# Attention in two passes, routing inside the second, and a recurrence whose input is added on VectorE

## The chip, the cores and the metric

The kernel runs on one core of one Trainium2 chip. The core has five engines with a queue each, which work side by side and wait for each other by semaphores: TensorE (PE in the profile; PEld is its loading of weights), VectorE (DVE), ScalarE (ACT), GpSimd (POOL) and SyncE (SP), which here only issues transfers. SBUF is the on-chip memory of 128 partitions, PSUM the memory that TensorE writes its sums to. The metric is device time in microseconds of one execution. Lower is better.

## The reference

Two layers over `x` of 4 x 2048 x 256 float32. What matters, cut:

```python
# layer 0
xn = layernorm(x); u = layernorm_w(xn) @ (Ws + Wi).T + bs + bi
h[t] = tanh(h[t-1] @ A.T + u[t])                 # 16 states, 2048 steps, per batch row
s = (h @ Wo.T + bo) * sigmoid(layernorm_w(xn) @ Wg.T + bg) + xn
g = silu(small per-feature MLP of xn)
x = x + s * g
# layer 1
xn = layernorm(x); q, k, v = xn @ Wq.T + bq, xn @ Wk.T + bk, xn @ Wv.T + bv
s = softmax_one(causal(q k^T / 4)) @ v           # 16 heads; it attends over the FIRST axis, the batch of 4
g = silu(MoE(xn))                                # 8 experts, top 2, capacity 2048, hidden 1024
x = x + s * g
```

The attention's sequence axis is the first one, so each of the 2048 positions attends among its 4 batch rows, and scores are ten products per position (4 + 3 + 2 + 1). The mixture gives each token's two experts a slot; the slot is the token's rank among the tokens that chose the expert, so a slot can be known only when all 8192 tokens have logits.

## The kernel before

All data of a stage is cut along the positions into NT = 16 tiles of 128 positions by 4 batch rows (1024 columns per partition). The stages are blocks with a barrier between them, each with an instruction list per engine written out by hand:

- `prepare`: loads and folds weights.
- `mix`, first loop: normalise, transpose, the recurrence's input `u_st`. Second loop (16 tiles): gate product `a_pG` (line 718), small MLP (lines 726, 728), output gates. Into its gaps the recurrence is woven: the 2048 steps are cut into 128 chains of 16, swept three times, which makes SWEEPS * L = 48 steps; slots 0 to 3 of the first twelve tiles take one each. A step is an identity product that copies `u_st` into PSUM (line 700), a product with the block-diagonal A added to it (703 or 706), and ScalarE's tanh into `h_st` (633). VectorE has no part in a step. Its list per tile: four instructions on the gate product (569), `finish` of the tile before (555, 557, 560), `normalise` (540), `units` (548).
- `recur`: more sweeps, only if the third one changed the last state.
- `attend`, one loop over 16 tiles, software-pipelined. `layer0(t)` on VectorE (956 to 972): layer 0's output times the gate, added to `x_st`, and its statistics. GpSimd's `scale` (909 to 917) makes the factors, ScalarE normalises (1046), SyncE stores the rows to HBM, TensorE turns them (1124), and from the turned tile makes Q (into `pY`), K (`pX`), the router's logits (1147) and V (`pY`). VectorE, for tile t: `layer0(t + 2)`, four products q * k (1003), four reductions to scores (1009), maximum (1014), subtraction (1017); then it waits for ScalarE's exponential (1096); sum, plus one, reciprocal, and `c_att` (1021 to 1029). GpSimd multiplies `c_att` by the values and adds, seven instructions per tile (936, 942) with a `scale` between them.
- `route`: a stage of its own, nearly all of it one list on VectorE: constants; `best`, `first`, one-hot of each token's two experts (1273 to 1282, the second choice without the lines for k == 0); a scan along the positions (1284); two TensorE products that count over partitions; places and slots (1291 to 1309); then 16 groups of three instructions over 128 x 1024 bfloat16 elements which write a slot's high part, low part and code as one-hots (1316 to 1319), each group followed by eight TensorE matmuls that add it into the table `d_ptab` (1351); last the table's decoding (1323 to 1333). SyncE meanwhile loads the first expert's weights.
- `experts`: 8 experts by 4 groups of 512 slots, gathered and scattered by GpSimd's indirect transfers.
- `combine`: the last gate and the store.

The order of each list is fixed, so an instruction waits for all ahead of it on its engine.

## Time and profile before

| | us |
|---|---|
| median of 3 runs | 1430.29 (1430.05 to 1431.13) |
| the profiled execution | 1429.75 |
| its span, first to last instruction | 1427.9 |
| mean granted TensorE clock | 0.935 of full |

| engine | busy us | share of the span |
|---|---|---|
| TensorE | 1175.3 | 82% |
| VectorE | 1016.6 | 71% |
| ScalarE | 628.1 | 44% |
| GpSimd | 625.2 | 44% |

The page shows these as rows, and the span in forty slices of 35.7 us, a digit for the busy tenths of each:

```profile
PE   4899999588888884146999989999899998999910
DVE  7757667759888887885767667676576765776638
POOL 5500000028777777013454544645546455464430
PEclk9999999799999997557999999999999999999965
```

Mix ends in the eighth slice, attention fills the next eight and a half, routing follows at half clock (5), and the experts begin at the end of the eighteenth. A view by windows gives the busy time of each engine in a stretch; a timeline gives the instructions in order of time, merged where neighbours are alike: start, duration from the first one's start to the last one's end, engine, line, what is written from what, the count, and in brackets the idle time before it with what ended it. A duration includes the time an instruction is held back once its engine has started it.

### The profile page before, as it was taken

To read this page: it belongs to the slowest core of one execution; us is meant where nothing else is said; L and a number is where in the kernel's file an instruction comes from. 1 tells how busy PE (TensorE), PEld (TensorE's weight loads), DVE (VectorE), ACT (ScalarE), POOL (GpSimd) and SP (SyncE) were. 2 spreads that over 40 slices of the span, in tenths; PEclk is the share of its full clock that TensorE was granted. 3 is DMA by queue.
4 is the path that set the end of the run, shared out by engine and by line. 5 is a ranking of instruction groups with operands and counts; after the bars stand their busy time and mean duration, and the time that the engine had idled before them with its cause. 6 is when DMAs were issued, how large, how long until landed. Compare 5 with 4: busy or idle time off the path is not lost. (4 is left out here: it accounts for less than half of the span.)

```text
span 1427.9 us, 22572 instructions
## 1 busy us (share of the span) xinstructions
PE 1175.3 (82%) x7547; PEld 802.9 (56%) x7547; DVE 1016.6 (71%) x1931; ACT 628.1 (44%) x960; POOL 625.2 (44%) x530
## 2 busy tenths in 40 slices
PE   4899999588888884146999989999899998999910
PEld 3566666366666663134566666666666665666610
DVE  7757667759888887885767667676576765776638
ACT  4855555233333441003544545445455454553522
POOL 5500000028777777013454544645546455464430
PEclk9999999799999997557999999999999999999965
DMA  8260000001111110105555445554555545555569
GB/s 328 83 214 1 1 1 1 15 30 31 31 31 31 32 31 16 59 19 109 105 109 104 76 99 101 112 106 71 108 92 113 109 66 114 89 111 104 66 168 347
DMA packets 148960, 122.55 MB, mean 86 GB/s; under 512 B 88400, under 2 KB 133328, under 8 KB 148720
## 3 DMA queue, kind: packets, MB, share of 16 engines
q1 hardware_dynamic: 114912, 83.90, 20.1%
q0 software_dynamic: 25200, 35.85, 16.4%
q10 hardware_dynamic: 8736, 1.33, 0.5%
q8 instruction: 68, 1.11, 0.3%
q14 instruction: 44, 0.36, 0.1%
HBM read 58.91 MB, written 44.30 MB: 72 GB/s over the span
## 5 line engine op out<-in xcount | busy, mean ns | idle before, releaser
L1722 ACT ACTIVATE e_h_all<-e_pH,e_b1c,e_h_scale 128x512 f32<-128x512 f32 x256 | 199.6, 780 | 283.9 <-PE e_pH L1763 256.1
L1777 PE MATMUL e_pY<-e_w_hi,e_h_hi 128*128 128x256 f16 x1024 | 279.6, 273 | 17.1 <-DVE e_w_lo L1597 10.0
L1506 POOL DMA_INDIRECT e_xg<-xn_rows,e_icol x140 | 162.4, 1160 | 287.1 <-DVE e_icol L1538 254.3
L1778 PE MATMUL e_pY<-e_w_lo,e_h_hi 128*128 128x256 f16 x1024 | 279.1, 273 | 0.0
L1779 PE MATMUL e_pY<-e_w_hi,e_h_lo 128*128 128x256 f16 x1024 | 279.1, 273 | 0.0
L1521 POOL DMA_INDIRECT expert_sums<-e_yo,e_dcol x128 | 213.0, 1664 | 76.7 <-issue 43.0
L1640 DVE TENSOR_TENSOR e_h_lo<-e_h_all,e_h_hi 128x512 f16<-128x512 f32 x256 | 177.3, 693 | 66.3 <-ACT e_h_hi L1722 56.6
L1761 PE MATMUL e_pH<-e_xT,e_w_hi 128*128 128x512 f16 x512 | 195.1, 381 | 26.5 <-DMA e_xT<-e_xs 17.6
L1762 PE MATMUL e_pH<-e_xT,e_w_hi 128*128 128x512 f16 x512 | 194.9, 381 | 0.0
L1763 PE MATMUL e_pH<-e_xT,e_w_lo 128*128 128x512 f16 x512 | 194.8, 380 | 0.0
L1777 PEld LDWEIGHTS e_pY<-e_w_hi,e_h_hi 128*128 128x128 f16 x1024 | 100.1, 98 | 42.9 <-DVE e_h_lo L1640 24.6
L1160 PE MATMUL c_pY<-late,c_xnT 128*128 128x256 f32 x512 | 117.9, 384 | 0.0
L1672 DVE SCALAR_TENSOR_TENSOR e_yo<-e_pY,e_y_scale,logit_st 128x512 f32<-128x512 f32 x64 | 48.1, 751 | 96.9 <-remote 67.2
L1160 PEld LDWEIGHTS c_pY<-late,c_xnT 128*128 128x128 f32 x512 | 98.9, 193 | 17.1 <-issue 0.3
L1778 PEld LDWEIGHTS e_pY<-e_w_lo,e_h_hi 128*128 128x128 f16 x1024 | 100.2, 98 | 14.4
L1779 PEld LDWEIGHTS e_pY<-e_w_hi,e_h_lo 128*128 128x128 f16 x1024 | 100.2, 98 | 11.6
L1722 ACT ACTIVATE e_h_hi<-e_pH,e_b1c,e_h_scale 128x512 f16<-128x512 f32 x128 | 99.0, 773 | 0.0
L1761 PEld LDWEIGHTS e_pH<-e_xT,e_w_hi 128*128 128x128 f16 x512 | 50.2, 98 | 81.9 <-issue 24.9
L904 POOL MEMSET c_mhalf<- 128x4 f32 x1 | 0.1, 102 | 211.6 <-POOLq L759 211.6
L1763 PEld LDWEIGHTS e_pH<-e_xT,e_w_lo 128*128 128x128 f16 x512 | 50.3, 98 | 61.0 <-issue 1.1
L1762 PEld LDWEIGHTS e_pH<-e_xT,e_w_hi 128*128 128x128 f16 x512 | 50.3, 98 | 60.6 <-issue 5.4
L1003 DVE TENSOR_TENSOR c_qk<-c_q,c_k 128x1024 f32<-128x1024 f32 (+1 forms) x64 | 71.7, 1179 | 0.0
(251 smaller groups left out, 2169.0 us busy)
## 6 DMA issues: line engine op xcount, KB each, us to landing
raw<-expert_w SPq DMA_DIRECT2D x18, 1024.0 KB
expert_sums<-a_zero SPq DMA_DIRECT2D x10, 1024.0 KB, 10.7
x_st<-x SPq DMA_DIRECT2D x16, 512.0 KB, 9.1
xn_rows<-c_xn SPq DMA_DIRECT2D x16, 512.0 KB, 3.0
f_ya<-expert_sums SPq DMA_DIRECT2D x16, 512.0 KB, 7.3
out<-x_st SPq DMA_DIRECT2D x8, 1024.0 KB, 8.5
e_xg<-xn_rows,e_icol POOLq DMA_INDIRECT x140
e_xT<-e_xs SPq DMA_TRANSPOSE x136
```

The lines of the kernel that those rows point to most:

```text
L1003: last = dve.tensor_tensor(qk[:, PAIR0[j]:PAIR0[j] + w, :], q[:, j:B, :], spread(k[u][:, j, :], w), ALU.mult)
L1160: last = pe.matmul(dst[:, b, :], xnT[:, kk, b * P:(b + 1) * P], v.wqkv[:, kk, n * D:(n + 1) * D], start=False, stop=(kk == KD - 1), skip_g ...
L1506: pool.indirect_dma_start(xg[:, q, 0:D + E], None, v.xn3_dram, bass.IndirectOffsetOnAxis(icol[u][:, q:q + 1], axis=0), bounds_check=N - 1, ...
L1521: pool.indirect_dma_start(v.y_dram, bass.IndirectOffsetOnAxis(dcol[u][:, q:q + 1], axis=0), yo[:, q, :], None, bounds_check=N + CAP - 1, o ...
L1640: dve.tensor_tensor(h_lo[:, h, :], h_all[h % 2][:, :], h_hi[:, h, :], ALU.subtract).then_inc(h_lo_ready, 1)
L1722: last = act.activation(dst, pH[h % NPH][:, :], ACT.Relu, bias=b1c[eu][:, h:h + 1], scale=h_scale[eu][:, 0:1])
L1761: pe.matmul(pH[h % NPH][:, :], w1_hi[:, k, rows], x_hi[:, k, :], start=(k == 0), stop=False)
L1762: pe.matmul(pH[h % NPH][:, :], w1_hi[:, k, rows], x_lo[:, k, :], start=False, stop=False)
L1763: last = pe.matmul(pH[h % NPH][:, :], w1_lo[:, k, rows], x_hi[:, k, :], start=False, stop=(k == KD - 1))
L1777: pe.matmul(pY[:, q, :], h_hi[:, h, cols], w2_hi[:, h, :], start=(h == 0), stop=False)
L1778: pe.matmul(pY[:, q, :], h_hi[:, h, cols], w2_lo[:, h, :], start=False, stop=False)
L1779: last = pe.matmul(pY[:, q, :], h_lo[:, h, cols], w2_hi[:, h, :], start=False, stop=(h == HT - 1))
```

## The change

In `mix`, a step's product with A stands alone (`start=True`); VectorE adds `u_st` to it into `r_in`, and ScalarE's tanh reads that. Step 0 reads `u_st` directly. `attend` becomes two loops. The first does everything that leads to logits: `layer0`, scaling, normalising, the row store, turning into `prod_st` (no longer into one `c_xnT`), logits. The second makes Q, K, V into three PSUM tiles, products, scores and weights, with `products(t + 1)` ahead of `weights(t)`, and the lines of `route` cut into pieces behind `weights(t)`: choosing in tiles 0 and 1, the scan in 2, places in 4, two groups of one-hots in each of tiles 5 to 12, decoding in 14. TensorE adds a group's one-hots to the table two tiles later, ahead of V. Constants and the splitting of the bias go from VectorE to GpSimd, into the first loop. GpSimd's scaling leaves its seven attention instructions. The stage `route` is gone; `h_st`, the normalised rows, routing's large arrays and the expert weights share one buffer, and some of the experts' arrays move into the memory of the late weights. The first load of expert weights is issued when the table is complete. Loops are written out, as before. The core of the diff:

```diff
 # mix, VectorE: a new step, called in slots 0 to 3 of a tile
+                def step(t, slot):
+                    for j, n, l in steps_at(t, slot):
+                        if j:
+                            if j >= 2:
+                                dve.wait_ge(state, j - 1)
+                            first = 1 if l == 0 else 0
+                            if first:
+                                dve.tensor_copy(rin[j % 2][:, 0:1], v.u_st[:, l, 0:1])
+                            dve.wait_ge(carried, j)
+                            dve.tensor_tensor(rin[j % 2][:, first:NCH], pR[j % 2][:, first:NCH], v.u_st[:, l, first:NCH],
+                                              ALU.add).then_inc(summed, 1)
...
                     last.then_inc(y_ready, 1)
+                    step(t, 0)
                     if t:
                         finish(t - 1)
+                    step(t, 1)
                     if t + 1 < NT:
                         if t:
                             dve.wait_ge(x_done, t)
                         normalise(t + 1)
+                        step(t, 2)
                         units(t + 1)
+                        step(t, 3)
...
 # mix, TensorE
-                        ins = pe.matmul(pR[j % 2], ident, v.u_st[:, l, :], start=True, stop=(j == 0),
-                                        skip_group_check=True)
...
+                            if l:
+                                ins = pe.matmul(pR[j % 2], v.at_blk, v.h_st[:, l - 1, :], start=True, stop=True)
...
 # attend, SyncE
+                for t in range(NT):
+                    sp.wait_ge(xn_ready, t + 1)
+                    sp.dma_start(dram_rows[t][:, :, 0:D], xn[t % 2]).then_inc(xn_out[t % 2], 16)
                 for u in range(2):
-                    sp.wait_ge(xn_out[u], 16 * NT // 2 + 16)
+                    sp.wait_ge(xn_out[u], 16 * NT // 2)
+                sp.wait_ge(table, 1)
+                sp.dma_start(v.raw[:, 0, :].rearrange("p (k h) -> p k h", k=KD),
+                             v.ew1[0].rearrange("(k p) h -> p k h", p=P)).then_inc(v.w1_in, 16)
...
 # attend, GpSimd: first all scaling, with the bias and the constants between
+                for t in range(NT):
+                    scale(t)
+                    if t == 2:
+                        pool.memset(ones3[:, :], 1.0).then_inc(bias_ready, 1)
+                        pool.tensor_copy(part3[:, 0, :], v.bqkv).then_inc(bias_ready, 1)
...
+                for t in range(NT):
+                    u = t % 2
+                    n = PV * t
+                    pool.wait_ge(v_evac, t + 1)
                     pool.wait_ge(att_ready, t + 1)
...
 # attend, VectorE
+                for t in range(NT):
+                    layer0(t)
...
+                def one_hots(n):
+                    m = n % 2
+                    if n >= 2:
+                        dve.wait_ge(used[m], n // 2)
+                    dve.tensor_tensor(ohh[m], counted, columns(hi, n), ALU.is_equal).then_inc(ohh_ready, 1)
+                    dve.tensor_tensor(ohl[m], counted, columns(lo, n), ALU.is_equal).then_inc(ohl_ready, 1)
+                    dve.wait_ge(ohh_ready, n + 1)
+                    dve.tensor_tensor(ohc[m], ohh[m], columns(code, n), ALU.mult).then_inc(ohc_ready, 1)
...
+                products(0)
+                scores(0)
+                for t in range(NT):
+                    if t + 1 < NT:
+                        products(t + 1)
+                    weights(t)
+                    if t < TOPK:
+                        if t == 0:
+                            dve.wait_ge(l_evac, NT)
+                            dve.wait_ge(xn_out[1], 16 * NT // 2)
+                        choose(t)
+                    elif t == 2:
+                        along()
+                    elif t == 4:
+                        places()
+                    for n in hots_of(t):
+                        one_hots(n)
+                    if t == HOTS_AT + K2 // NB // HOTS + 1:
+                        tables()
+                    if t + 1 < NT:
+                        scores(t + 1)
...
 # attend, TensorE
+                for t in range(NT + 2):
+                    if t + 2 < NT:
+                        output(t + 2)
+                    if t < NT:
+                        turn(t)
+                    if 0 <= t - 1 < NT:
+                        logits(t - 1)
+                    if 0 <= t - 2:
+                        turn_logits(t - 2)
+
+                pe.wait_ge(bias_ready, 9)
+                pe.wait_ge(op_ready, NT)
...
+                            for h in hots_of(t - 2):
+                                pe.wait_ge(ohl_ready, h + 1)
+                                pe.wait_ge(ohc_ready, h + 1)
+                                for a in range(WIDE):
+                                    for i in range(INNER_N):
+                                        last = pe.matmul(ptab, ohl[h % 2][:, a, :, i], ohc[h % 2][:, a, :, i],
+                                                         start=False, stop=False, skip_group_check=True)
+                                last.then_inc(used[h % 2], 1)
```

Here `choose`, `along`, `places` and `tables` hold the lines of `route` for the choice of an expert, the scan, the places and slots, and the decoding; `products`, `scores` and `weights` hold attention's own lines 1003, 1009 to 1017 and 1021 to 1029.

## Rows read from the trace of the kernel before

**Rows 1.** Stage windows: stretch, length, busy (PE, PEld, DVE, ACT, POOL), clock, DMA share, GB/s.

```profile
100.00:264.00 164.00, 162.90 (x760) 104.45 (x758) 109.05 (x199) 89.25 (x143) 0.00 (x0) 1.00 0.00 1
598.10:627.60 29.50, 16.53 (x120) 12.72 (x120) 29.00 (x49) 0.00 (x0) 0.00 (x0) 0.50 0.00 0
```

**Rows 2.** The timeline of TensorE, one tile of mix (start, us, instruction).

```profile
103.50 3.62 PE L718 MATMUL a_pG<-first,prod_st 128*128 128x256 f32 x16
106.95 0.38 PE L700 MATMUL a_pT<-u_st,cst 128*128 128x128 f32 x2
107.17 0.39 PE L703 MATMUL a_pT<-h_st,late 128*128 128x128 f32 x2
113.34 0.38 PE L700 MATMUL a_pT<-u_st,cst 128*128 128x128 f32 x2
116.39 3.62 PE L718 MATMUL a_pG<-first,prod_st 128*128 128x256 f32 x16
```

**Rows 3.** VectorE in the same tile; last a group by line and shape.

```profile
107.15 1.66 DVE L569 SCALAR_TENSOR_TENSOR prod_st<-a_pG,a_again,first 128x256 f32<-128x256 f32 x4 [3.36 <-PE a_pG L718]
112.25 1.38 DVE L540 TENSOR_SCALAR a_xn<-x_st,a_mv,a_r 128x256 f32<-128x256 f32 x4
L523 DVE TENSOR_TENSOR u_st<-a_pGU,a_ag 128x128 f32<-128x128 f32 x8 | 2.3, 291 | 0.3
```

**Rows 4.** The timeline of VectorE, a steady attention tile.

```profile
449.37 0.42 DVE L1029 TENSOR_TENSOR c_att<-c_ex,c_mx 128x256 f32<-128x256 f32 x1
459.15 3.00 DVE L1009 TENSOR_REDUCE c_sc<-c_qk 128x64 f32<-128x1024 f32 x4
464.86 0.60 DVE L1021 TENSOR_REDUCE c_mx<-c_ex 128x64 f32<-128x256 f32 x1 [1.39 <-ACT c_ex L1096]
466.31 0.43 DVE L1029 TENSOR_TENSOR c_att<-c_ex,c_mx 128x256 f32<-128x256 f32 x1
```

**Rows 5.** VectorE, then GpSimd, in the last two attention tiles.

```profile
550.26 7.67 DVE L1003 TENSOR_TENSOR c_qk<-c_q,c_k 128x1024 f32<-128x1024 f32 x4
550.42 2.85 POOL L936 TENSOR_TENSOR prod_st<-c_att,c_v 128x1024 f32<-128x1024 f32 x1 [4.23 <-DVE c_att L1029]
564.73 1.93 POOL L936 TENSOR_TENSOR prod_st<-c_att,c_v 128x1024 f32<-128x1024 f32 x1 [2.70 <-DVE c_att L1029]
571.73 1.26 POOL L942 TENSOR_TENSOR prod_st<-prod_st,c_pv 128x512 f32<-128x512 f32 x1 [0.18 <-POOL c_pv L936]
573.97 0.72 POOL L942 TENSOR_TENSOR prod_st<-prod_st,c_pv 128x256 f32<-128x256 f32 x1 [0.18 <-POOL c_pv L936]
```

**Rows 6.** Routing: one group by line, then VectorE's timeline.

```profile
L1316 DVE TENSOR_TENSOR d_ohh<-d_iota,d_hi 128x1024 bf16<-128x1024 bf16 x16 | 11.0, 687 | 0.4 <-DVE d_lo L1309 0.4
577.70 0.67 DVE L1273 TENSOR_REDUCE d_best<-logit_st 128x64 f32<-128x512 f32 x1
587.47 2.29 DVE L1284 TENSOR_TENSOR_SCAN d_pos<-d_within,d_hot 128x1024 f32<-128x1024 f32 x1
591.27 0.23 DVE L1291 COPY d_total<-d_ptot 128x64 f32<-128x64 f32 x1 [1.26 <-PE d_ptot L1342]
```

**Rows 7.** The start of attention: VectorE, TensorE, ScalarE.

```profile
281.72 1.23 DVE L956 TENSOR_TENSOR prod_st<-c_pX,prod_st 128x1024 f32<-128x1024 f32 x1
286.01 0.38 DVE L972 BATCH_NORM_AGGREGATE c_mv<-c_st 128x2 f32<-128x6 f32 x4 [0.26 <-DVE c_st L964]
301.36 3.00 DVE L1003 TENSOR_TENSOR c_qk<-c_q,c_k 128x1024 f32<-128x1024 f32 x4
269.76 2.08 PE L1114 MATMUL c_pX<-late,h_st 64*128 64x512 f32 x4 [6.61 <-PEq L759]
280.88 1.97 PE L1124 MATMUL c_pT<-cst,c_xn 128*128 128x128 f32 x8 [5.65 <-ACT c_xn L1046]
294.51 1.02 ACT L1070 ACTIVATE c_k<-c_pX 128x1024 f32<-128x1024 f32 x1 [2.86 <-PE c_pX L1160]
```

**Rows 8.** The timeline of VectorE, the experts' first instruction.

```profile
631.48 0.17 DVE L1538 COPY e_icol<-idx 128x4 int32<-128x4 int32 x1 [0.62 <-PEq L1243]
```

More of the change, by code:

```diff
@@ L208, in program @@
         attend(nc, v)
+        experts(nc, v)
         front.close()
[L210 to L218 removed]
         combine(nc, v)
@@ L353, in _ @@
                 linked(dve.tensor_tensor(v.gconst[0:M, :], pk[0:M, 0:1], first[0:M, W_B2:W_B2 + 1], ALU.add))
-def tiles(eng, body):
-    for t in range(NT):
-        body(t // 2, t % 2, NT - 1 - t)
 def mix(nc, v):
@@ L1354, in _, with output @@
-                pe.matmul(ptab[:, 0:P], ident16[:, :], zero16[:, :], start=False, stop=True,
-                          skip_group_check=True).then_inc(table, 1)
+                def output(t):
+                    if t >= 2:
+                        pe.wait_ge(op_ready, t - 1)
+                    for n in range(2):
+                        half = slice(2 * GRP * n, 2 * GRP * n + 2 * GRP)
+                        last = pe.matmul(pO[t % 2][:, 2 * n:2 * n + 2, :].rearrange("p b d -> p (b d)"),
+                                         v.h_st[half, t, :],
+                                         v.wo_pad[half, 2 * n:2 * n + 2, :].rearrange("p b d -> p (b d)"),
+                                         start=True, stop=True)
+                    last.then_inc(o_done, 1)
@@ new lines, in turn, with logits @@
+                def turn(t):
+                    pe.wait_ge(xn_ready, t + 1)
+                    if t:
+                        pe.wait_ge(t_evac, t)
+                    for kk in range(KD):
+                        for b in range(B):
+                            last = pe.transpose(pT[:, kk, b * P:(b + 1) * P], xn[t % 2][:, b, kk * P:(kk + 1) * P], ident)
+                    last.then_inc(t_done, 1)
+                def logits(t):
+                    pe.wait_ge(t_evac, t + 1)
+                    if t >= 2:
+                        pe.wait_ge(l_evac, t - 1)
+                    for kk in range(KD):
+                        for b in range(B):
+                            last = pe.matmul(pL[t % 2][GRP * b:GRP * b + GRP, 0:P], v.wgr[:, kk, :],
+                                             xnT(t)[:, kk, b * P:(b + 1) * P], start=(kk == 0), stop=(kk == KD - 1))
+                    last.then_inc(l_done, 1)
```

770 lines of the change are left out of this document (349 added, 421 removed).

## The prediction

> **What bounds the kernel now.** I read the page's forty slices first: VectorE and TensorE are both busy nearly everywhere, so shares don't decide and each stage has to be read from its own limit. Then I read the stage windows. In the second half of mix (100 to 264 us) TensorE is busy 162.90 of 164 us [rows 1] and one tile of time takes 12.89 us, from one gate product to the next [rows 2]: TensorE is the bound there. Next comes attention (269.7 to 574.7). The timeline of VectorE for one steady tile runs from one `c_att` to the next in 16.94 us, and the only long hole is 1.39 us waiting for ScalarE's exponential [rows 4]: VectorE is the bound. But its busy time is not all work. In the last tiles, where nothing but the products, scores and weights is left, the four products take 7.67 us [rows 5], while the very first four took 3.00 [rows 7]. What differs is GpSimd: in the first case it multiplies attention by values at the same moment, and its own first instruction takes 2.85 us where the one of the last tile, with VectorE idle, takes 1.93 [rows 5]. So the two engines take turns, an instruction each. Last comes routing: from 577.70 to 631.48 VectorE works alone, with 48 one-hot instructions of 0.60 us pitch (29.00 us busy in 29.5) as the largest part and TensorE at half clock beside it [rows 1, 6, 8]. GpSimd is idle all through it.
>
> **Part 1, the recurrence's input (mix).** Each of 48 steps loses an identity product: the pair starts at 106.95, the next matmul at 107.17 [rows 2], so 0.22 us of TensorE per step, 0.88 per tile with four steps, twelve tiles: 10.6 us at most. What is late next is a chain that now runs through VectorE. The add reads PSUM and SBUF, as `u_st` does at 291 ns [rows 3]. In a tile VectorE starts on the gate product at 107.15, is done at about 108.75, adds for step 0 (about 0.3), then goes through `finish`, which took until 112.25, so about 3.5 us [rows 3], adds for step 1 and lets ScalarE take its tanh (0.4): about 6.4 us behind the gate's end at 106.95. TensorE would want to start step 2 at 113.34 less the two identity pairs ahead of it, 5.95 behind. It waits 0.4 to 0.5. From step 2 to the next gate product it needs 3.05 (113.34 to 116.39) less two pairs, 2.6, and the gate itself 3.45 [rows 2]: 6.4 + 2.6 + 3.4 = 12.4 instead of 12.89. I take 0.55 per tile and a little from the first step: **7 us** gained. Both ends: 10.6 if the adds slip in unseen, 3 if each of the four adds costs a further wait.
>
> **Part 2, attention's first pass.** It starts where the old one does (first output product 269.76, VectorE from 271.9). VectorE needs for one `layer0` from 281.72 to 286.01 and 0.38, so 4.67 us [rows 7]; with the added wait 4.8. Sixteen make 77. The bias's splitting (5 us on VectorE before) and the constants move to GpSimd, nine instructions or so of at most the 1.93 us of its 1024-wide one; only one instruction of a `layer0` has two SBUF inputs and can be made to wait, in four or five tiles: 0 to 8 us, taken as 3. The tiny scaling instructions add 2. Sum **82 us**, to 353.9. Lower end 75. Upper end: TensorE is at half clock when the pass starts; there one output product takes 2.08 and one turning 1.97 [rows 7], and logits with their turning back at most another turning, 6.0 per tile, 96 in all if the clock never rose; rows of one stage can't say whether it does, and I end the range at 93.
>
> **The drain between the passes** is new idle time on VectorE. Behind the last `layer0`: scaling on GpSimd 2, normalising 2.1, turning 2, evacuation 1, logits and their round trip 2.5 to 3, so 10; then Q and K of tile 0, from their start 2 us behind the end of turning at 280.88 + 1.97 to K's evacuation at 294.51 in the old kernel, about 11 with the clock low at first; then 1 for the evacuation. The first product starts 22 us behind the pass: 376. In the old kernel it started at 301.36 [rows 7]. Tile 0 has to wait for Q and K of tile 1 besides, since `products(1)` stands ahead of `weights(0)`: its `c_att` comes 16.5 later, at 392.5. All this could be 6 less with the clock high.
>
> **Part 3, the second pass.** VectorE's own work per tile: products 3.00 [rows 7], scores from 459.15 to 463.47 (464.86 less the 1.39 of idling), 4.3 with maximum and subtraction, 0.2 of it waiting, so 4.1; weights from 464.86 to the end of `c_att` at 466.74, 1.9 [rows 4]: 9.0. The exponential's 1.39 is hidden now, behind `products(t+1)`. GpSimd starts a tile when `c_att` is written, and alone takes from 564.73 to 573.97 + 0.72, **9.96 us**, of which 8.9 are its seven instructions [rows 5]. TensorE has three products like the gate's of 3.45 [rows 2], with a bias each: under 12. What counts is the taking of turns: each VectorE instruction with two SBUF inputs that finds GpSimd in one lets it end first, and GpSimd then gets in before the next one. (a) A plain tile: `scores` comes first and is mostly reductions, which the rows show untouched (3.00 at 459.15 with GpSimd busy); the four products meet GpSimd's third to sixth instruction, 3.9 us of waiting, bounded by 0 and by the 4.67 of the row [rows 5]: 12.9. (b) A tile with two groups of one-hots (t = 5 to 12): six instructions of 0.60, placed right behind `c_att`, so exactly where GpSimd's largest ones start. Five of GpSimd's get in between; the first five last from 564.73 to 571.73 + 1.26, 8.3, without gaps 7.5, and about 0.1 is saved at each change of hands: 6.6. Then 9.0 + 3.6 + 6.6 = **19.2**. The other end is 12.6, no waiting. Nothing in the old trace pairs these bfloat16 instructions with a busy GpSimd; the nearest row is the float32 pair of the products, 7.67 against 3.00, and I take it. The Trainium skill, page SBUF — State Buffer, section Who interferes with whom, makes no difference of type here: an instruction of VectorE with two SBUF inputs and one of GpSimd that reads SBUF share a read port and the second blocks until the first is done. By that rule the sum stays at 19.2 per tile; by a reading in which 16-bit operands leave room it would be about 14.5. (c) Choosing: from 577.70 to 587.47, 9.8 for both experts [rows 6], mostly two-input instructions; tiles 0 and 1 together 18.0 + 9.8 + 8.9 waiting = 36.7. (d) Scan and copy 2.5 in tile 2: 16.1. (e) Places, from 591.27 to the one-hots at 598.1, 6.8 in tile 4: 21.5. (f) Tile 14 with the tables, no products left: 9.7. Sum from tile 0's `c_att` to tile 15's: 36.7 + 16.1 + 21.5 + 2 x 12.9 + 8 x 19.2 + 9.7 = 263. Without any waiting it would be 182, with GpSimd's 8.9 added to each of fifteen tiles 316. The same bookkeeping on the old tile gives 16.7 where 16.94 was measured, 1.4% short, so 4 us more: 267. GpSimd's last tile adds 10, the stage boundary 0.6.
>
> **Part 4, the separate routing stage** is gone: GpSimd's tail of 10 us, the boundary, and 56 us to the experts' first instruction at 631.48 [rows 8]. The expert weights' first load now waits for the table and the last row store; the table is complete some 30 us before the stage ends, and the load needed 8 us, so it stays hidden; with the cover gone it would cost those 8. The experts are unchanged, only placed elsewhere in SBUF: 0.
>
> **The sum.** 392.5 + 267 + 10 + 0.6 = 670.1 for the experts' first instruction against 631.48, so 38.6 later; less 7 from mix: 31.6. The profiled execution took 1429.75 us (span 1427.9), 0.5 below the median 1430.29, the same within the runs. **1429.75 + 31.6 = 1461.5.** Its own range, from the bounds that belong to it (mix 3 to 10, pass one -7 to +11, drain -6, one us either way in each of the eight one-hot tiles): 1446 to 1478.
>
> **The rivals.** *A, as above:* routing's instructions change hands with GpSimd. For it: both engines' rows of tile 14 lengthen in step. Chance 0.64. *B, the one-hots don't wait,* the rest does (the faster side): eight tiles at 14.5 instead of 19.2, 38 less, **1424**. For it: their bfloat16 form is twice as fast per element as the float32 one, a mode that no row shows beside GpSimd. Against it: both operands lie in SBUF, as in the products. It decides for a gain when the wait per one-hot tile falls below about 2.6 us. Chance 0.12. *C, hardly any of routing waits:* tiles 0 to 4 too at their own work, 17 less again, **1407**; against it are float32 instructions of the very kind of the rows. Chance 0.06. *D, A with a slow TensorE on top:* with 3.1 us of fast matmuls in a tile of 4.8 the clock may fall back in pass one, and in the one-hot tiles TensorE idles for over 5 us in one piece; 12 to 22 more, about **1477**. The rows of mix and old attention show the high clock under nearly full load only, and the routing stage stayed at 0.50 while busy 16.53 of 29.5 [rows 1]. Chance 0.12. The Trainium skill, page TensorE: Matmul & The Clock Gate, section What's actually happening, has the throttled clock as the default which activity releases; by it this case would be likelier than I make it. *E, between A and B,* four in five of the one-hots' waits gone or overlapped by luck of position: **1430**. Chance 0.06. That the change leaves mix untimed (adds slower than the identity) moves each by +7, inside the ranges.
>
> **The numbers.** A measurement of this kernel can tell about 0.2% (2.9 us) from no change. Slower: A and D, 0.76. Same: E, 0.06. Faster: B and C, 0.18. The range reaches from B's time to the upper part of D, 1422 to 1484, leaving out C, a bit of B and the tail of D, some 0.16. The likeliest case's own range is 1446 to 1478.
>
> **What would show it.** Mix's tile at 12.3 to 12.5 us instead of 12.89. Pass one at about 5.1 per tile on VectorE. A hole of some 20 us on VectorE between the passes. One-hot instructions recorded at 0.69 beside an idle GpSimd but at 1.5 to 2.5 each in the second pass, and `c_att` to `c_att` near 19 in tiles 5 to 12 and 13 in tiles 3 and 13; if those tiles show 14.5, B holds and the forecast fails there. Experts starting near 663. TensorE's granted clock in 272 to 370 tells D from A.

## The result, and the profile after

| | median us | runs from to | ratio to before |
|---|---|---|---|
| before | 1430.17 | 1428.97 to 1431.13 | |
| changed | 1455.01 | 1452.37 to 1456.37 | 1.0172, interval 1.0154 to 1.0189 |

The change costs 24.8 us; the forecast was 31.6. The profiled execution took 1454.48 us with a span of 1452.6. I read it in the same order as before: first mix, then the two passes, then the experts' start.

Stage windows of the changed kernel. The columns are stretch, length, busy time of PE, PEld, DVE, ACT and POOL, granted clock, DMA share, GB/s. The stretches are the second half of mix, pass one, the hole behind it, and the one-hot tiles of pass two.

```profile
96.00:258.00 162.00, 159.66 (x694) 96.18 (x690) 119.63 (x245) 92.82 (x146) 0.00 (x0) 1.00 0.00 1
264.00:341.00 77.00, 49.16 (x403) 27.49 (x400) 67.97 (x160) 47.01 (x100) 46.14 (x79) 0.87 0.33 102
341.00:357.00 16.00, 13.40 (x106) 10.39 (x105) 0.15 (x1) 7.06 (x15) 1.16 (x2) 1.00 0.22 53
460.00:617.00 157.00, 120.37 (x537) 96.60 (x538) 154.38 (x161) 26.07 (x31) 87.07 (x56) 0.82 0.04 14
```

TensorE still bounds mix (159.66 of 162 us). In the one-hot tiles VectorE does (154.38 of 157), and TensorE is far from full. TensorE's timeline in mix, two gate products in a row, answers [rows 2]:

```profile
101.94 3.62 PE L735 MATMUL a_pG<-first,prod_st 128*128 128x256 f32 x16
114.25 3.62 PE L735 MATMUL a_pG<-first,prod_st 128*128 128x256 f32 x16
```

That is 12.31 us per tile where it was 12.89. VectorE's timeline between the passes answers [rows 7]. It shows the last statistics of pass one, the first products of pass two, and tile 0's `c_att`:

```profile
338.51 0.38 DVE L1063 BATCH_NORM_AGGREGATE c_mv<-c_st 128x2 f32<-128x6 f32 x4
356.85 3.03 DVE L1076 TENSOR_TENSOR c_qk<-c_q,c_k 128x1024 f32<-128x1024 f32 x4 [17.96 <-ACT c_k L1268]
...
368.48 3.03 DVE L1076 TENSOR_TENSOR c_qk<-c_q,c_k 128x1024 f32<-128x1024 f32 x4 [4.48 <-ACT c_k L1268]
...
372.87 0.43 DVE L1108 TENSOR_TENSOR c_att<-c_ex,c_mx 128x256 f32<-128x256 f32 x1
```

The square bracket is idle time and who ended it: two holes, 17.96 and 4.48 us, both ended by ScalarE's evacuation of K. Next comes a whole one-hot tile of VectorE, from `c_att` to `c_att`, which answers [rows 4] for the tile and [rows 6] for the one-hots:

```profile
479.20 0.42 DVE L1108 TENSOR_TENSOR c_att<-c_ex,c_mx 128x256 f32<-128x256 f32 x1
479.77 2.47 DVE L1179 TENSOR_TENSOR shared<-d_iota,d_hi 128x1024 bf16<-128x1024 bf16 x1
482.16 1.98 DVE L1180 TENSOR_TENSOR shared<-d_iota,d_lo 128x1024 bf16<-128x1024 bf16 x1
484.06 2.29 DVE L1182 TENSOR_TENSOR shared<-shared,d_code 128x1024 bf16<-128x1024 bf16 x1
...
490.44 2.99 DVE L1084 TENSOR_REDUCE c_sc<-c_qk 128x64 f32<-128x1024 f32 x4
...
494.43 3.02 DVE L1076 TENSOR_TENSOR c_qk<-c_q,c_k 128x1024 f32<-128x1024 f32 x4
...
498.81 0.42 DVE L1108 TENSOR_TENSOR c_att<-c_ex,c_mx 128x256 f32<-128x256 f32 x1
```

The same instruction took 0.687 in the old routing stage [rows 6]. GpSimd beside it, for the same tile (compare the 1.93 and 1.26 of an undisturbed tile in [rows 5]):

```profile
479.75 1.93 POOL L1033 TENSOR_TENSOR prod_st<-c_att,c_v 128x1024 f32<-128x1024 f32 x1 [8.26 <-DVE c_att L1108]
481.77 1.82 POOL L1033 TENSOR_TENSOR c_pv<-c_att,c_v 128x768 f32<-128x768 f32 x1
483.67 2.14 POOL L1038 TENSOR_TENSOR prod_st<-prod_st,c_pv 128x768 f32<-128x768 f32 x1
```

Read the two together. GpSimd's first instruction ends at 481.68 and VectorE's first one-hot at 482.24, though both could start at 479.7. GpSimd's third ends at 485.81, and VectorE's third at 486.35. Each engine is let in when the other ends, one instruction at a time. The six one-hots take 10.7 us where 3.7 would do. By the time the products come (3.02, as quick as alone) GpSimd has finished. Lastly the experts' first instruction, which answers [rows 8]:

```profile
655.13 0.17 DVE L1562 COPY e_icol<-late 128x4 int32<-128x4 int32 x1 [10.14 <-PEq L950]
```

It starts 23.65 us later than before. Everything behind it takes 1.1 us longer. So nearly all of the loss lies ahead of the experts.

### The profile page after: what moved, and what is told of

It reads as the page before. It is cut to its first block and busy times, and to the rows that moved or that the text cites. A ratio compares the mean times of both kernels' runs of the same rounds, so it can differ in the third digit from the quotient of the medians.

```text
span 1452.6 us, 22136 instructions
## 1 busy us (share of the span) xinstructions
PE 1191.6 (82%) x7451; PEld 807.3 (56%) x7451; DVE 1072.0 (74%) x1962; ACT 630.3 (43%) x960; POOL 624.4 (43%) x548
## 5 line engine op out<-in xcount | busy, mean ns | idle before, releaser
L1803 PE MATMUL e_pY<-e_w_hi,late 128*128 128x256 f16 x1024 | 279.9, 273 | 0.0
L1530 POOL DMA_INDIRECT e_xg<-xn_rows,e_icol x140 | 151.0, 1078 | 295.0 <-DVE e_icol L1562 262.2
L1545 POOL DMA_INDIRECT expert_sums<-late,e_dcol x128 | 212.7, 1662 | 81.6 <-issue 47.2
L1664 DVE TENSOR_TENSOR late<-e_h_all,e_h_hi 128x512 f16<-128x512 f32 x256 | 177.3, 693 | 66.4 <-ACT e_h_hi L1746 60.5
L1696 DVE SCALAR_TENSOR_TENSOR late<-e_pY,e_y_scale,logit_st 128x512 f32<-128x512 f32 x64 | 48.1, 751 | 95.6 <-remote 56.1
L1802 PEld LDWEIGHTS e_pY<-e_w_lo,e_h_hi 128*128 128x128 f16 x1024 | 100.5, 98 | 14.7
L1803 PEld LDWEIGHTS e_pY<-e_w_hi,late 128*128 128x128 f16 x1024 | 100.5, 98 | 12.1 <-issue 0.2
L1033 POOL TENSOR_TENSOR prod_st<-c_att,c_v 128x1024 f32<-128x1024 f32 x16 | 30.9, 1932 | 133.7 <-DVE c_att L1108 117.2
L1038 POOL TENSOR_TENSOR prod_st<-prod_st,c_pv 128x768 f32<-128x768 f32 (+2 forms) x48 | 75.0, 1562 | 3.8
L1076 DVE TENSOR_TENSOR c_qk<-c_q,c_k 128x1024 f32<-128x1024 f32 (+1 forms) x64 | 54.2, 908 | 23.3 <-ACT c_k L1268 23.3
```

The source lines that it names most:

```text
L1038: pool.tensor_tensor(o, o, part, ALU.add).then_inc(pv_step, 1)
L1076: last = dve.tensor_tensor(qk[:, PAIR0[j]:PAIR0[j] + w, :], q[:, j:B, :], spread(k[:, j, :], w), ALU.mult)
L1530: pool.indirect_dma_start(xg[:, q, 0:D + E], None, v.xn3_dram, bass.IndirectOffsetOnAxis(icol[u][:, q:q + 1], axis=0), bounds_check=N - 1, ...
L1545: pool.indirect_dma_start(v.y_dram, bass.IndirectOffsetOnAxis(dcol[u][:, q:q + 1], axis=0), yo[:, q, :], None, bounds_check=N + CAP - 1, o ...
L1664: dve.tensor_tensor(h_lo[:, h, :], h_all[h % 2][:, :], h_hi[:, h, :], ALU.subtract).then_inc(h_lo_ready, 1)
L1802: pe.matmul(pY[:, q, :], h_hi[:, h, cols], w2_lo[:, h, :], start=False, stop=False)
```

## The experiments

All ratios are to the kernel before, timed on the same chip in the same rounds.

### Mix's part alone

In the old kernel, only the recurrence's input is moved:

```diff
-                        ins = pe.matmul(pR[j % 2], ident, v.u_st[:, l, :], start=True, stop=(j == 0),
-                                        skip_group_check=True)
...
-                            ins = pe.matmul(pR[j % 2], v.at_blk, v.h_st[:, l - 1, :], start=False, stop=True,
-                                            skip_group_check=True)
...
+                                ins = pe.matmul(pR[j % 2], v.at_blk, v.h_st[:, l - 1, :], start=True, stop=True)
...
+                            dve.tensor_tensor(rin[j % 2][:, first:NCH], pR[j % 2][:, first:NCH], v.u_st[:, l, first:NCH],
+                                              ALU.add).then_inc(summed, 1)
```

> The kernel before with only the recurrence's change: VectorE adds the input, the identity product is gone. Attention and routing stay as they were. Theory: the gain seen in mix of the changed kernel (attention starts 6.6 us earlier) is worth the same at the end, since attention is bound by VectorE from its start: about 6.5 us less than before, some 1423.5. Rival: the gain is swallowed at the start of attention (its first product waits for something else that mix sets, the last row stores or the state check), then the time is that of before, 1430. Mix's tile 12.3 us from gate product to gate product in both.

Measured: 1421.7 us (1421.55 to 1422.79), ratio 0.9941, interval 0.9925 to 0.9958. The experts' first instruction lies at 624.25 instead of 631.48, 7.2 earlier, so mix's gain arrives whole: attention's VectorE starts 6.0 earlier, and 1.2 more comes by tile 0's `c_att`. It also means that the rest of the change costs 33 us, not 25.

### Two passes, routing behind them

```diff
                     weights(t)
-                    if t < TOPK:
...
-                        choose(t)
...
-                    for n in hots_of(t):
-                        one_hots(n)
                     if t + 1 < NT:
                         scores(t + 1)
...
+                choose(0)
+                choose(1)
+                along()
+                places()
+                for n in range(K2 // NB):
+                    one_hots(n)
+                tables()
```

TensorE's counting and table products move behind its loop in the same way.

> The changed kernel with two passes, but every instruction of the routing (choosing, scan, places, one-hots, tables, and TensorE's table products) behind the second loop instead of inside it. Theory (what costs is that the routing's two-input instructions take turns with GpSimd inside the loop): all fifteen tiles of the second pass show the 13.4 us that tiles 3 and 13 show now, 202 us from tile 0's c_att to tile 15's instead of 271.7; then some 54 us of routing at 0.6 per one-hot instruction, about 4 more where it meets GpSimd's last tile, and up to 5 for the first experts' weights if their load isn't hidden. Experts' first instruction near 633 to 638, total 1433 to 1438, about 20 less than the changed kernel and about the time of before. Rival (the extra cost is routing's own work and the two passes themselves, turn-taking is small): then it moves work only, and the time stays within 5 of 1455.

Measured: 1437.53 us (1436.4 to 1442.94), ratio 1.0058, interval 1.0037 to 1.0079. From tile 0's `c_att` to tile 15's it is 197.4 us: 13.72 for the first tile, 13.40 to 13.44 for each of the others and 9.16 for the last. The list of waits names the one new cost outside the passes, the experts waiting for their first weights (columns: who waited for what, us in total, times, longest):

```profile
DVE e_b1c L1563 <- DMA shared<-expert_w: 5.4, 1, 5.4
```

So two passes as such, with the routing apart, are 16 us slower than the old arrangement with the same mix (1437.5 against 1421.7): the experts' first instruction comes 10.1 later (634.33 against 624.25), and these weights add 5.4 behind it. Weaving the routing in, which should have won time and does hide that load, loses another 17.5.

### The same pieces in another place

The one edit is the place of `weights(t)`:

```diff
                         products(t + 1)
-                    weights(t)
...
                     for n in hots_of(t):
                         one_hots(n)
...
+                    weights(t)
                     if t + 1 < NT:
                         scores(t + 1)
```

> The changed kernel with one move in VectorE's list: the routing's piece of tile t stands ahead of weights(t), behind products(t + 1), instead of right behind weights(t). Nothing is added or removed. Theory: weights(t) releases GpSimd, so a piece right behind it meets GpSimd's seven instructions, and a piece ahead of it meets an idle GpSimd; then only the products wait (3.9 us as in a plain tile) and one-hot tiles take 9.0 + 3.6 + 3.9 to 4.5, about 17 us instead of 19.6. With the other pieces that is some 22 us less, about 1433. One-hot instructions recorded near 0.69 and not 1.5 to 2.5. Rival (place doesn't matter: whoever is late is made up for, since GpSimd has 8.9 us of work per tile that must be paired with something on VectorE): within 5 of 1455.

Measured: 1434.05 us (1431.09 to 1436.23), ratio 1.0025, interval 1.0014 to 1.0036. One-hot tiles take 17.04 us each instead of 19.61. The timeline of VectorE in one:

```profile
487.53 0.60 DVE L1089 TENSOR_REDUCE c_mx<-c_sc 128x64 f32<-128x256 f32 x1
488.17 2.00 DVE L1092 TENSOR_TENSOR c_ex<-c_sc,c_mx 128x256 f32<-128x256 f32 x1
490.09 5.91 DVE L1076 TENSOR_TENSOR c_qk<-c_q,c_k 128x1024 f32<-128x1024 f32 x4
495.92 0.68 DVE L1179 TENSOR_TENSOR shared<-d_iota,d_hi 128x1024 bf16<-128x1024 bf16 x1
496.52 0.68 DVE L1180 TENSOR_TENSOR shared<-d_iota,d_lo 128x1024 bf16<-128x1024 bf16 x1
```

Nothing was added or removed. The one-hots now cost their own 0.60 apiece, while the subtraction (2.00, alone 0.42) and the products (5.91, alone 3.03) do the waiting. The rival, that GpSimd's work must be paid for in any place, is out: 21 us came from the place alone.

### GpSimd's instructions cut short

Each of GpSimd's seven instructions of a tile works on 16 columns. The kernel leaves out nearly all of the product of attention and values; the routing, which reads nothing of it, stays the same.

```diff
-                        w = B - j
-                        a = att[u][:, j, j:B, :].unsqueeze(3).broadcast_to([P, w, H, DK])
...
-                        o = v.prod_st[:, t, j * D:B * D]
...
+                        a = att[u][:, j, j, 0:1].broadcast_to([P, DK])
...
+                        o = v.prod_st[:, t, j * D:j * D + DK]
```

> The changed kernel with GpSimd's seven attention instructions of a tile cut to 16 columns each, same count, same waits. It leaves out nearly all of the product of attention and values, so attention's result is wrong; the experts and all other stages do the same work. Theory (GpSimd's instructions are what holds up VectorE's): one-hot instructions fall to 0.68 each and tiles 5 to 12 to VectorE's own work, or to what TensorE needs for a tile if that is more, 13 to 14.5 instead of 19.6; plain tiles below 13.4; GpSimd's tail of 10 us gone. Second pass 271.7 down to about 205, total near 1380. Rival (TensorE's falling clock or the order of the lists sets the tiles): tiles 5 to 12 stay over 17 and the total within 25 of 1455.

Measured once: 1368.6 us. Tiles 5 to 12 take 12.7 to 13.6, and the high parts of the one-hots in them 0.69 to 0.75 each. The window from 460 to 560 shows what the bound is then (columns as above):

```profile
460.00:560.00 100.00, 96.28 (x491) 81.81 (x489) 89.66 (x151) 25.26 (x30) 23.54 (x54) 1.00 0.07 22
```

TensorE, 96.28 of 100 us at the full clock. So it was GpSimd's instructions that held VectorE up, and TensorE's own limit is some 13 us a tile, well below the 19.6.

### The ramp in PSUM

```diff
-                counted = iota[:, :, :].unsqueeze(1).broadcast_to([P, WIDE, P, INNER_N])
+                ramp = pL[0][:, 2 * P:3 * P]
+                counted = ramp.unsqueeze(1).unsqueeze(3).broadcast_to([P, WIDE, P, INNER_N])
...
+                            linked(dve.tensor_copy(ramp, v.iota))
```

> The changed kernel with the one-hots' ramp read from PSUM, a float32 copy, instead of from SBUF in bfloat16. So the first two of each group's three instructions have one input in SBUF only; alone they take longer, an estimate of 1.1 instead of 0.6. Their place in the list is the same. Theory (two inputs in SBUF are what makes an instruction wait for GpSimd): only the third of each group waits, the others show 1.1 to 1.2 each beside a busy GpSimd; own work of a one-hot tile rises by 2.0, waiting falls from 7 to about 2.5, tiles 5 to 12 at 17.1 to 17.7, total about 1438. Rival (any VectorE instruction that reads SBUF waits): 2.0 more on top in each, tiles at 21.6, total 1471.

Measured: 1432.22 us (1427.34 to 1437.18), ratio 1.0018, interval 1.0002 to 1.0034. Tiles 5 to 12 take 16.27 us. VectorE in one of them, right behind `c_att`, with GpSimd busy:

```profile
496.72 1.23 DVE L1180 TENSOR_TENSOR shared<-c_pL,d_hi 128x1024 bf16<-128x1024 f32 x1
497.87 1.22 DVE L1181 TENSOR_TENSOR shared<-c_pL,d_lo 128x1024 bf16<-128x1024 f32 x1
499.00 1.77 DVE L1183 TENSOR_TENSOR shared<-shared,d_code 128x1024 bf16<-128x1024 bf16 x1
```

The form that is nearly twice as slow alone is quicker here: only its second input comes from SBUF, and it takes 1.21 to 1.23 beside GpSimd and 1.21 alone (in the kernel with both remedies, below). Only the coded part waits (1.77, then 1.18). The ramp's type changed with its place, but type alone is not what frees an instruction: the products are float32 with both inputs in SBUF, and they wait (5.91 against 3.03 above). I had the direction and was 1 us a tile too high: I allowed 2.5 of waiting in a tile and there is 1.6, all of it in the coded parts. The subtraction and the products run clear, since GpSimd is through at 506.80 and they start at 507.70.

### The kinds of instruction, measured by themselves

Why did the tables in tile 14 cost so much? Four extra instructions that multiply 128x128 float32 by a constant stand in the hole and in plain tiles, once reading SBUF and once PSUM:

```diff
+                def kinds(src):
+                    for _ in range(4):
+                        linked(dve.tensor_scalar(empty[:, :], src, 1.0, None, ALU.mult))
+                kinds(v.cst[:, 0:P])
+                dve.wait_ge(l_evac, NT)
+                kinds(pL[0][:, 0:P])
...
+                    elif t == 3:
+                        kinds(v.cst[:, 0:P])
+                    elif t == 13:
+                        kinds(pL[0][:, 0:P])
```

> The changed kernel with four extra one-input instructions (multiply by a constant, 128x128 float32 into SBUF, the kind of the tables' shifts) at each of four places: from SBUF and from PSUM in the hole between the passes with GpSimd idle, from SBUF right behind weights(3), from PSUM right behind weights(13), where GpSimd works. Asks why the tables cost 8 us in tile 14 and 1.95 behind an idle GpSimd. Theory: the kind that reads one SBUF operand and writes SBUF waits for GpSimd too: 0.1 to 0.2 each in the hole, 1 to 2 each behind weights(3), so tile 3 some 6 longer; from PSUM they stay at 0.1 to 0.2 in both places, tile 13 about 1 longer. Rival (one-input instructions never wait, and tile 14 had another cause): 0.2 or less at all four places, tile 3 about 1 longer.

VectorE's timeline at the four places, in order of time: SBUF in the hole, PSUM in the hole, SBUF behind `weights(3)`, PSUM behind `weights(13)`. The second number is the time of all four instructions:

```profile
344.30 1.05 DVE L1203 TENSOR_SCALAR d_empty<-cst 128x128 f32<-128x128 f32 x4
353.78 1.27 DVE L1203 TENSOR_SCALAR d_empty<-c_pL 128x128 f32<-128x128 f32 x4 [8.44 <-ACT logit_st L1258]
431.35 6.59 DVE L1203 TENSOR_SCALAR d_empty<-cst 128x128 f32<-128x128 f32 x4
624.62 1.27 DVE L1203 TENSOR_SCALAR d_empty<-c_pL 128x128 f32<-128x128 f32 x4
```

Measured once: 1460.7 us. One input in SBUF is enough to wait, if the instruction is of this kind: 6.59 instead of 1.05. From PSUM it is 1.27 in both places. The second half of my expectation fell: tile 3 did not grow by 6, only from 13.44 to 15.60, and tile 13 by 0.2 instead of 1. The 5.5 us of waiting in the four instructions took GpSimd forward, so the subtraction and the products behind them, which wait 4.4 us in a plain tile, ran clear (0.42 and 3.02).

### Choosing in the hole

```diff
+                dve.wait_ge(l_evac, NT)
+                dve.wait_ge(xn_out[1], 16 * NT // 2)
+                choose(0)
+                choose(1)
                 products(0)
                 scores(0)
+                along()
```

> As the run before, and the choosing of both experts is done ahead of products(0), in the hole of 18 us in which VectorE waits for tile 0's K, the scan behind scores(0) in the next hole. Theory: choosing with GpSimd idle takes 9.8 us, which lies wholly inside the hole of 17.96; so tiles 0 and 1 fall from 36.7 to about 27, tile 2 to 13.5: 10 less than the run before, about 1423, 7 less than the kernel before. Rival: the hole isn't free, because choosing needs the last logits (their evacuation and turning), which arrive only near its end: then the gain is about half, 1428.

"The run before" is the kernel with the pieces ahead of `weights(t)`. Measured: 1422.07 us (1421.53 to 1425.11), ratio 0.9949, interval 0.993 to 0.9968. Tile 0's `c_att` ends at 376.05 instead of 383.07, tile 1 takes 13.73 instead of 17.61, tile 2 is plain, and `products(0)` starts at 360.98, within 0.1 of the run before. The choosing did start late, at 351.16, when the last logits were there, as the rival had it, but its 9.8 us still fitted.

### The choice split

```diff
+                for t0, t1 in ((0, 12), (12, NT)):
+                    dve.wait_ge(l_evac, t1)
+                    choose(0, t0, t1)
+                    choose(1, t0, t1)
+                dve.wait_ge(xn_out[1], 16 * NT // 2)
+                along()
+                places()
                 products(0)
                 scores(0)
```

> As the kernel with the choosing in the hole, and the choosing is cut in two by tiles: twelve tiles' logits as soon as these are there, right behind the first pass, the last four when theirs come; scan and places follow ahead of products(0), and tile 4 is a plain tile. Its temporaries lie where nothing of the first pass is still read. Theory: the choosing starts 7 us earlier and costs 1 us more for the cut; scan and counting end near 357, places (6.8) by 365.5, products(0) and scores(0) by 372.5, 1.3 later than now; tile 4 falls from 20.33 to 13.43. Net 5.5 less than the kernel with the unsplit choosing: about 1416.5, 1% below before. Rival (the small cut instructions cost nearly what whole ones do, and the waits between places and TensorE's counts open a new hole): nothing gained, 1422.

Measured: 1418.31 us (1417.8 to 1421.03), ratio 0.9913, interval 0.9897 to 0.993. Tile 4 is plain, as expected. The gain of 3.8 is less than 5.5, since the cut choice takes 13.2 us (345.77 to 358.98) where the whole one took 9.8: its second part, a quarter of the tiles, still has thirteen instructions of 0.17 to 0.38 and four of 0.19. In this execution pass one also ended 2.6 later, at 344.2.

### Both remedies at once

```diff
-                counted = iota[:, :, :].unsqueeze(1).broadcast_to([P, WIDE, P, INNER_N])
+                ramp = pL[0][:, 2 * P:3 * P]
+                counted = ramp.unsqueeze(1).unsqueeze(3).broadcast_to([P, WIDE, P, INNER_N])
...
-                    weights(t)
...
+                    weights(t)
                     if t + 1 < NT:
```

> The kernel with the pieces ahead of weights(t) and, at once, the ramp from PSUM: both remedies together. Theory (each only takes away waiting for GpSimd, and in the late place there is none to take away): the one-hots are late and run alone, so the form from PSUM only costs its longer time, four instructions a tile at 1.13 instead of 0.60, and the products wait as before: tiles 5 to 12 at 19.2 instead of 17.04, total about 1451, 17 more than with the late place alone. Rival (the two remedies add up, or the PSUM form is better wherever it stands): at or below 1434.

Measured: 1451.92 us (1447.99 to 1452.81), ratio 1.0148, interval 1.0133 to 1.0164; tiles 5 to 12 at 19.16. Against the changed kernel one remedy wins 21 us alone, the other 23, and together they win 3. The first one-hot of a tile, with GpSimd idle:

```profile
479.74 1.21 DVE L1180 TENSOR_TENSOR shared<-c_pL,d_hi 128x1024 bf16<-128x1024 f32 x1
```

The next one starts at 480.87. So it is 1.13 us from start to start where the form from SBUF needs 0.60, four times a tile, and the products wait in both. The form from PSUM is not better in itself.

### Each kind in its place

```diff
                     if t + 1 < NT:
                         products(t + 1)
+                    coded(hots_of(t))
...
                     weights(t)
+                    high_low(hots_of(t + 1))
                     if t + 1 < NT:
                         scores(t + 1)
```

`high_low` writes the high and low parts with the ramp from PSUM, `coded` multiplies by the code.

> As the kernel with the split choosing, and the one-hots are parted by kind: the high and low parts take their ramp from PSUM (one input in SBUF, 1.13 apart instead of 0.60) and stand right behind weights(t), beside GpSimd's seven instructions; the coded part (two inputs in SBUF) stands ahead of weights(t), where GpSimd is idle. Theory: four parts of 1.13 and the reductions (3.6) cover 8.1 of GpSimd's 8.9 us without a wait, so products and coded parts run alone; a one-hot tile takes 9.0 + 4.5 + 1.2 and up to 1 of waiting, 15.0 to 15.7 instead of 17.04, eight of them 11 to 16 us less: total 1402 to 1407. Rival (in 17.04 TensorE is as near its limit as VectorE, or the tile waits for its table products, since the low part now comes 4 us behind the coded part of the group before): tiles stay near 17, total 1418.

Measured: 1404.83 us (1403.45 to 1407.73), ratio 0.9826, interval 0.9813 to 0.984. Tiles 5 to 12 take 15.48. VectorE and then GpSimd in one of them:

```profile
467.24 2.35 DVE L1192 TENSOR_TENSOR shared<-c_pL,d_hi 128x1024 bf16<-128x1024 f32 x2
469.51 2.34 DVE L1196 TENSOR_TENSOR shared<-c_pL,d_lo 128x1024 bf16<-128x1024 f32 x2
471.77 2.99 DVE L1085 TENSOR_REDUCE c_sc<-c_qk 128x64 f32<-128x1024 f32 x4
474.80 0.60 DVE L1090 TENSOR_REDUCE c_mx<-c_sc 128x64 f32<-128x256 f32 x1
475.43 0.67 DVE L1093 TENSOR_TENSOR c_ex<-c_sc,c_mx 128x256 f32<-128x256 f32 x1
476.02 3.55 DVE L1077 TENSOR_TENSOR c_qk<-c_q,c_k 128x1024 f32<-128x1024 f32 x4
```

```profile
467.23 1.94 POOL L1034 TENSOR_TENSOR prod_st<-c_att,c_v 128x1024 f32<-128x1024 f32 x1 [6.03 <-DVE c_att L1109]
...
475.89 0.79 POOL L1039 TENSOR_TENSOR prod_st<-prod_st,c_pv 128x256 f32<-128x256 f32 x1
```

GpSimd's seven instructions run from 467.23 to 476.68, and in all that time VectorE issues nothing that could wait but the subtraction and the first product, which lose 0.8 us between them. This kernel is 50 us faster than the changed one and 25 faster than the one before.

## Why the prediction was right, and where its terms were off

**The direction and the mechanism held.** The forecast was 1461.5 us, with 1446 to 1478 as the range of its likeliest case; the measured time is 1455.01. It said slower because each routing instruction with two inputs in SBUF, placed right behind `c_att`, takes turns with GpSimd. All of it can be put in one account. VectorE's own work in a one-hot tile is 12.6 us by the forecast's terms (9.0 + 3.6), or 14.7 with the ramp in PSUM (9.0 + 4 x 1.13 + 2 x 0.60). What is over is waiting:

| tiles 5 to 12 | tile us | own | waiting |
|---|---|---|---|
| changed kernel | 19.61 | 12.6 | 7.0 |
| pieces ahead of `weights(t)` | 17.04 | 12.6 | 4.4 |
| ramp in PSUM | 16.27 | 14.7 | 1.6 |
| both | 19.16 | 14.7 | 4.5 |
| each kind in its place | 15.48 | 14.7 | 0.8 |

The 9.0 and 3.6 are the forecast's terms, not measured apart, but where single instructions can be added up they agree: in the changed kernel the six one-hots take 11.1 us against 6 x 0.687, which is 7.0 over. GpSimd's work is the same in all five rows, so the waiting is not a fixed price of that work. It is that part of it that finds nothing beside it but instructions that wait. Rivals B and E (one-hots of 16-bit data don't wait) fell: 2.47, 1.98 and 2.29 against 0.687 [rows 6]. C fell with them. The rule of the Trainium skill, page SBUF — State Buffer, section Who interferes with whom, on two SBUF inputs, is borne out in bfloat16 too, by the same three numbers.

**Step by step.**

- *Mix.* Forecast 12.4 a tile and 7 in all. Measured 12.31, and attention's VectorE starts 6.6 earlier (265.3 against 271.9). Right, and the mix-only kernel shows it at the end as well.
- *Pass one: the term was too large.* Forecast 82 us with 4.8 per `layer0`. The last `layer0` ends at 338.9, so 74. I took 4.67 from a row that held 0.26 of idling in front of the aggregate and gaps of its own [rows 7], then added to it; in the steady pass a `layer0` follows the last one every 4.38, and sixteen times 0.42 is 6.7 of the 8. The 5 us for GpSimd's bias and scaling fell too: the one instruction that could wait took at most 1.39 instead of 1.23. In their place stand three holes that wait for TensorE's output product, 1.81, 1.29 and 0.32.
- *The drain: too large by 4.* Forecast 22, and 38.5 to tile 0's `c_att`. Measured 17.96, and 34.4. I had priced it with TensorE's clock low and said 6 less if high. The window from 341 to 357 shows the clock at 1.00.
- *Pass two without its last tile: right.* Tiles 0 and 1 together 36.7 (forecast 36.7), tile 2 15.83 (16.1), tiles 3 and 13 13.44 and 13.48 (12.9), tile 4 20.74 (21.5), one-hot tiles 19.62 (19.2).
- *Tile 14: the step that failed in its reasoning.* Forecast 9.7, measured 14.58. I counted the tables at their duration alone. VectorE in that tile:

```profile
630.93 1.62 DVE L1190 TENSOR_SCALAR late<-d_tab 128x128 int32<-128x128 int32 x1
632.47 0.21 DVE L1191 TENSOR_SCALAR d_found<-d_tab 128x128 int32<-128x128 int32 x1
632.72 1.47 DVE L1192 SCALAR_TENSOR_TENSOR late<-late,d_found 128x128 int32<-128x128 int32 x1
634.22 1.78 DVE L1194 TENSOR_SCALAR d_found<-d_tab 128x128 int32<-128x128 int32 x1
```

  The first of these in the kernel with the pieces ahead of `weights(t)`, where GpSimd is idle:

```profile
611.93 0.23 DVE L1190 TENSOR_SCALAR late<-d_tab 128x128 int32<-128x128 int32 x1
```

  There the tables' tile is 1.95 longer than a plain one (15.38 against 13.43). Beside a busy GpSimd they take 8.0, from 630.58 to 638.53. And of the six that compute, three have one input only: the forecast let nothing wait but instructions with two. The four-places experiment shows the kind by itself, 1.05 against 6.59. The Trainium skill, page SBUF — State Buffer, section Who interferes with whom, has it: it lists the multiply-or-shift-by-a-constant among the forms that may take the second, shared access even with a single input, and reductions among those that never do. The traces agree with both halves, the second by the reductions of `scores`, 3.00 in the hole and 2.99 beside a busy GpSimd. I had used the rule on two inputs from that section and passed over this one.
- *Tail, boundary, experts.* Forecast 10.6 and 0, measured 10.14 from the last `c_att` to the experts' first instruction, and 1.1 behind it.

In sum: mix's extra 0.4 the wrong way, pass one 8 less, the drain 4 less, pass two 4.7 more than 267, the tail 0.5 less. From the forecast of 663 for the experts' first instruction that gives 655.5, and the trace has 655.1. Two terms were 12 us too large together and one was 4.7 too small, so part of the closeness of the total is luck. The 4.7 would be 8.3 without the 4 us that the forecast added for what its bookkeeping missed in the old tile: 4.9 in tile 14 and 3.3 in the eight one-hot tiles. Two slips of its arithmetic change nothing here: 1429.75 + 31.6 is 1461.35, and the bounds that it names, added straight, give 1437 to 1484, more than its 1446 to 1478.

**The slow clock (rival D) did not decide, but it is there.** The forecast named the granted clock from 272 to 370 as the sign that tells D from A; it was 0.92, and 1.00 in the drain. In pass two it did fall, to 0.82 from 460 to 617, yet TensorE waited for the one-hots, as the list of waits of the changed kernel has it for that stretch (us in total, times, longest):

```profile
PE c_pL L1359 <- DVE shared L1182: 42.9, 16, 13.1
```

The longest, with 3.1 more, falls in the first of the eight tiles. TensorE's timeline in a later one:

```profile
506.11 1.10 PE L1359 MATMUL c_pL<-shared 128*128 128x128 bf16 x8 [0.65 <-DVE shared L1182]
510.27 1.10 PE L1359 MATMUL c_pL<-shared 128*128 128x128 bf16 x8 [3.06 <-DVE shared L1182]
```

In the seven later tiles it waits 3.3 to 4.5 us each, so a faster TensorE would only have waited longer. In pass one it costs a little, and differs between executions of the same instructions. The stretch from 300 to 341 in the changed kernel (columns as in the windows above):

```profile
300.00:341.00 41.00, 26.29 (x264) 15.51 (x265) 37.31 (x90) 30.01 (x67) 21.09 (x37) 1.00 0.42 127
```

The same stretch of the kernel with the split choice, whose pass one has the same instructions:

```profile
300.00:341.00 41.00, 31.20 (x257) 17.71 (x257) 34.02 (x81) 26.58 (x59) 15.39 (x32) 0.83 0.40 120
```

The pass ended at 338.9 in the first and at 344.2 in the second, with holes on VectorE that wait for TensorE's output product. The list of waits of the second has this for the stretch (columns as before), and 3.5 us more for `c_pX`:

```profile
DVE prod_st L1053 <- PE c_pY L1312: 3.7, 2, 2.5
```

In the other kernels with this pass it ended between 340.1 and 344.3. So the profile of the changed kernel shows the pass at its shortest, and 74 us is the lower end of 74 to 79. What makes the clock fall in one execution and not in another was not tried.

**What the change really bought and paid.** From the medians, in us, each against the one before it: mix's part -8.5; two passes with the routing apart +16; routing into the second pass behind `weights(t)` +17.5. How the 10.1 us that two passes lose ahead of the experts divide between the new holes (17.96 and 4.48) and the rest was not tried. The same routing ahead of `weights(t)` gives back 21, choosing in the hole 12, the split 4, the one-hots parted by kind 13.5.

## What to carry to other kernels

Before work is woven into another stage's loop, write down for each instruction whether it can wait for the neighbour engine, and put those that can where the neighbour is idle; those that can't (reductions, one operand in PSUM) go beside it. The busy shares, 71% for VectorE and 44% for GpSimd, told nothing of this. A form that is slower alone, like the ramp from PSUM, can be the faster one in that place, and cost 18 us in another, so form and place have to be chosen together.

## What the runs showed of the hardware

- A VectorE instruction with one SBUF input and an SBUF output (128x128, multiply by a constant) waits for GpSimd: 1.05 us for four alone, 6.59 for four beside it. With its input in PSUM: 1.27 in both places.
- Reductions beside a busy GpSimd take what they take alone: the four of `scores` 2.99 with each kind in its place, and 3.00 in the hole between the passes.
- The one-hot at 128x1024 into bfloat16 has a pitch of 0.60 with both inputs bfloat16 in SBUF, and 1.13 with the ramp as float32 in PSUM.
- Waiting is not additive. 5.5 us of waiting added to a plain tile lengthened it by 2.2, own work included, since the later instructions then ran clear.
